# Where the head pieces and three attention units stand in the expert stages of a two-layer hybrid transformer kernel

## The chip, the cores and the metric

The kernel runs on one core of a Trainium2 chip, in one launch. The metric is the device time of that core in microseconds (us), lower is better. TensorE multiplies and transposes, VectorE and ScalarE work elementwise and empty the PSUM banks, GpSimd does a few powers and masks, and a queue of its own issues the transfers.

## The reference

Four sequences of 256 tokens of width 256 pass through eight residual blocks, each behind a layer norm:

```python
x = x + L0_attn_a(norm(x))   # 16 heads, causal softmax attention on a latent key/value
x = x + L0_ffn(norm(x))      # experts: top 2 of 8, shared W1/W3/W2 with a low-rank part per expert
x = x + L0_attn_b(norm(x))   # per token, softmax over the 16 heads of the same token
x = x + L0_ffn(norm(x))      # the experts again
x = x + L1_attn_a(norm(x))   # gated delta rule (linear attention)
x = x + L1_ffn(norm(x))      # gelu
x = x + L1_attn_b(norm(x))   # 16 heads, causal attention, one key/value head
x = x + L1_ffn(norm(x))
```

The parts that matter here are `L0_ffn` (gated product `silu(x W1 + lora) * (x W3 + lora)`, once per chosen expert slot), `L0_attn_b` (`scores[s, h, t] = q[s, h] . k[s, t]` for the 16 heads of one token, softmax over `t`, then a weighted sum of the 16 value rows) and `L0_attn_a`.

## The kernel before

All data of one sequence stays in SBUF. The work is cut into named stages such as `x_first` or `head_scores`. `program` calls the stages in one order written out by hand, and each engine walks that same order and issues only its own instructions of each stage. So every engine's queue is in order, and a stage's place decides what is queued behind it on every engine that has a part in it. Semaphores tie the engines together. PSUM has 8 banks. `lanes` tells which of them a stage may claim, and a claim waits until the bank's last user has drained it.

`experts(stage, k, s, beside)` computes the experts of sequence `s`. FT is 7. For step m = 0 to 8 it runs `x_first` m (m < 7), then the stages placed at slot `f<m>`, then `x_second` m-2 (m > 1), then (inside `middle`, from m = 4) `down_sum`, then the stages placed at slot `m`. `x_first` m is 16 TensorE instructions into a bank, a silu on ScalarE (line 1317) and a product on VectorE (line 1713). `x_second` m adds 8 TensorE instructions to the same bank and has a silu and a product of its own, and that product frees the bank. Two silu buffers are used in turn, so the silu of one product waits for the product two before it. After step 8 come `down` 1 0 (slot `down10`) and `down` 1 1, 14 TensorE instructions each; `down` 1 0 needs the products of all `x_second`.

`token_heads(s)` places `L0_attn_b` of another sequence beside those experts: `norm_t` 2 (transposes of the normed rows, waiting for VectorE's norm), `heads_in` (TensorE projects q, k, v; VectorE rotates them, lines 1755 to 1763), then 16 pieces of VectorE work. Pieces 0 to 7 are `head_scores` (a 128x1024 product and a 128x1024 sum, lines 1770 and 1771), pieces 8 to 15 are `head_mix` (lines 1787 and 1788). Pieces 3 and 7 end the scores of a token tile: they add a maximum and a subtraction (1774, 1775) and an Exp on ScalarE (1339). Pieces 8 and 12 start with a sum and a reciprocal (1785, 1786), and 11 and 15 end with a scaling (1791). `head_out_t` at slot `down10` waits for piece 15. There are four such stages, two per call of `middle`: the heads of the even sequences 0 and 2 beside the first-layer experts of 1 and 3, and the heads of the odd sequences 1 and 3 beside the second experts of 0 and 2. In the even ones the call order ahead is `x_first` 0, `lora`, `norm_x` 2, `experts`; in the odd ones other work lies between `norm_x` 2 and `norm_t` 2. `x_first` has banks 0 to 3 here.

The border half is one call of `experts` for sequence 2 (c) beside the four attention units of sequence 3 (d): `scores` (TensorE, maxima on VectorE, 8 Exp instructions on ScalarE, line 1266), `weights` (12 transposes, copies by VectorE and ScalarE), `values`, `values_t`. There `x_first` has only banks 0 to 2, so `x_first` m+1 waits for the product of `x_second` m-2, and sequence d uses banks 3 to 7. Exp and silu need different tables on ScalarE, so each change between them has a table load.

Of the kernel before, what the change touches and what calls it, by code (L numbers as in the profile page):

```python
# [97 lines left out]
def hybrid_kernel(nc, x_in, masks, packs, where, out):  # L98
    with ExitStack() as ctx:
# [319 lines left out]
        def program(stage):  # L419
# [24 lines left out]
            a, b, c, d = range(4)  # L444
# [15 lines left out]
            for other in (("scores", 0, (d, 0)), ("weights", 0, (d, 0)), ("spread_t", 0, c), ("top_exp", 0, c),  # L460
# [1 line left out]
                          ("gates", 0, c)):  # L462
                stage(*other)
            experts(stage, 0, c, {"f1": [("weights", 0, (d, 1))],
                                  "f2": [("values", 0, (d, 1)), ("scores", 0, (d, 2))],
                                  2: [("values_t", 0, (d, 1))], "f3": [("weights", 0, (d, 2))],
                                  3: [("values", 0, (d, 2)), ("scores", 0, (d, 3))],
                                  "f4": [("values_t", 0, (d, 2))], 4: [("weights", 0, (d, 3))],
                                  "f5": [("values", 0, (d, 3))], 5: [("values_t", 0, (d, 3))],
                                  6: [("out_in", 0, d)], 7: [("out_proj", 0, d), ("norm_x", 1, d)],  # L470
                                  "down00": [("norm_t", 1, d), ("router", 0, d), ("top_exp", 0, d), ("gates", 0, d)],
                                  "down01": [("spread_t", 0, d)], "down10": [("spread", 0, d), ("spread2", 0, d)]})
            halves[0] = False
# [23 lines left out]
        def middle(stage, a, b):  # L497
# [3 lines left out]
            stage("lora", 0, a)  # L501
            stage("norm_x", 2, a)
            experts(stage, 0, b, token_heads(a))
            stage("router", 1, a)
            stage("lora", 0, b)
# [5 lines left out]
            stage("x_first", 1, (a, 0))  # L511
            stage("gates", 1, a)
            experts(stage, 1, a, token_heads(b))
            stage("router", 1, b)
            stage("lora", 1, a)
# [50 lines left out]
        def token_heads(s):  # L566

            pieces = [("head_scores", 0, (s, a, h)) for a in range(NT) for h in range(HP)] \
                + [("head_mix", 0, (s, a, h)) for a in range(NT) for h in range(HP)]
            beside = {"f0": [("norm_t", 2, s)], 0: [("heads_in", 0, s)]}  # L570
            slots = ["f1", 1, "f2", 2, 2, "f3", 3, "f4", 4, 4, "f5", 5, 5, "f6", 6, 7]
            for slot, piece in zip(slots, pieces):
                beside.setdefault(slot, []).append(piece)
            beside["down10"] = [("head_out_t", 0, s), ("head_out", 0, s), ("norm_x", 3, s)]
            beside["down11"] = [("norm_t", 3, s)]
            return beside

        def experts(stage, k, s, beside):

            def others(slot):  # L580
                for b in beside.get(slot, ()):
                    stage(*b)

            for m in range(FT + 2):
                if m < FT and (m or (k == 0 and s % 2 == 0)):
                    stage("x_first", k, (s, m))
                others(f"f{m}")
                if m >= 2:
                    stage("x_second", k, (s, m - 2))
                if weave[0] and m >= 4:  # L590
                    summing[0] = True
                    for n in range(0 if m == 4 else m - 2, m - 1):
                        stage("down_sum", k, (s, n))
                others(m)
            for i in range(TOPK):
                for a in range(NT):
                    stage("down", k, (s, i, a))
                    others(f"down{i}{a}")
            summing[0] = False
            stage("lora_t", k, s)  # L600
# [69 lines left out]
        def _(pe):  # L670
# [554 lines left out]
            def stage(name, k, s):  # L1225
                seq = s if isinstance(s, int) else s[0]
                ring.lane = lanes(name, k, seq)
                table[name](k, s)

            program(stage)  # L1230


        @block.scalar
        def _(act):
# [259 lines left out]
            act.dma_start(pk[1][:, :], packs[1]).then_inc(loaded[1], 16)  # L1494
            act.dma_start(raw, masks).then_inc(masks_loaded, 16)
            program(lambda name, k, s: table[name](k, s))


        @block.vector
        def _(dve):  # L1500
# [586 lines left out]
            for s in range(S):  # L2087
                dve.memset(Vp[s][:, :, :, HD:HD + 1], 1.0).then_inc(prep, 1)
                dve.memset(Vp[s][:, :, :, HD + 1:PW], 0.0).then_inc(prep, 1)

            program(lambda name, k, s: table[name](k, s))


# [185 lines left out]
```

## Time and profile before

| | before |
|---|---|
| median of 3 runs | 1358.17 us (1352.16 to 1358.5) |
| profiled execution, its own time | 1358.74 us |
| its span | 1356.6 us |
| TensorE busy | 1214.7 us, 90% |
| VectorE busy | 747.1 us, 55% |
| ScalarE busy | 416.3 us, 31% |
| mean granted TensorE clock | 0.974 |

The span is the stretch that the profiler recorded; the execution's own time is 2.1 us longer. Busy shares are means over stages with different limits. An idle time in a timeline row stands in brackets with the engine that ended it. Ends of pipelined matmuls are modelled, so lengths of TensorE work are best read from start to start.

### The profile page before, as it was taken

To read this page: it belongs to the slowest core of one execution; us is meant where nothing else is said; L and a number is where in the kernel's file an instruction comes from. 1 tells how busy PE (TensorE), PEld (TensorE's weight loads), DVE (VectorE), ACT (ScalarE), POOL (GpSimd) and SP (SyncE) were. 2 spreads that over 40 slices of the span, in tenths; PEclk is the share of its full clock that TensorE was granted. 3 is DMA by queue.
4 is the path that set the end of the run, shared out by engine and by line. 5 is a ranking of instruction groups with operands and counts; after the bars stand their busy time and mean duration, and the time that the engine had idled before them with its cause. 6 is when DMAs were issued, how large, how long until landed. Compare 5 with 4: busy or idle time off the path is not lost.

```text
span 1356.6 us, 17608 instructions
## 1 busy us (share of the span) xinstructions
PE 1214.7 (90%) x6865; PEld 920.4 (68%) x6865; DVE 747.1 (55%) x1725; ACT 416.3 (31%) x897; POOL 79.7 (6%) x69
## 2 busy tenths in 40 slices
PE   6889898989999999978787898989989999999788
PEld 5577474766867778767665774756658777787666
DVE  5743387795456446444634333886964474564452
ACT  3522020222322343333453421212213322433352
POOL 0000000000110120010000000000002102200100
PEclk9999898999999989999998999999989999999999
DMA  8200000000000000000000000000000000000000
GB/s 351 98 1 0 0 1 0 1 0 0 1 0 1 1 1 1 1 1 9 1 8 1 0 1 0 0 1 0 0 1 1 1 0 1 0 1 2 1 1 16
DMA packets 3569, 17.32 MB, mean 13 GB/s; under 512 B 288, under 2 KB 2464, under 8 KB 2976
## 3 DMA queue, kind: packets, MB, share of 16 engines
q1 hardware_dynamic: 2912, 14.12, 2.6%
q10 hardware_dynamic: 576, 2.08, 0.4%
q8 instruction: 55, 0.90, 0.3%
q14 instruction: 26, 0.21, 0.0%
HBM read 15.15 MB, written 1.05 MB: 12 GB/s over the span
## 4 chain that ended last, share of the span: by engine, by line
PE 58%; DVE 22%; issue 9%; ACT 7%; POOL 3%; DMA 0%; DVEq 0%; POOLq 0%; ACTq 0%
PE bank L672 53%; ACT scr L1266 3%; DVE scr L1771 3%; DVE scr L1770 2%; DVE scr L1788 2%; PE bank L689 2%; DVE scr L1787 2%; DVE XnT L1944 1%; DVE scr L1713 1%; DVE XnT L1946 1%; DVE scr L1540 1%; DVE stat L1532 1%; POOL rstd L2100 1%; ACT L1317 1%; DVE negmax L1622 1%
## 5 line engine op out<-in xcount | busy, mean ns | idle before, releaser
L672 PE MATMUL bank<-pack,scr 128*128 128x512 f32 (+2 forms) x944 | 310.7, 481 | 8.5 <-ACT scr L1244 7.5
L672 PE MATMUL bank<-XnT,pack 128*128 128x256 f32 x1024 | 257.4, 392 | 16.5 <-ACT XnT L1244 7.1
L672 PEld LDWEIGHTS bank<-pack,scr 128*128 128x128 f32 x944 | 177.2, 192 | 115.6 <-issue 90.7
L672 PE MATMUL bank<-scr,pack 128*128 128x256 f32 x944 | 234.9, 390 | 19.3 <-DVE scr L1713 18.0
L672 PEld LDWEIGHTS bank<-XnT,pack 128*128 128x128 f32 x1024 | 195.5, 195 | 51.9 <-ACT XnT L1244 9.6
L672 PEld LDWEIGHTS bank<-scr,pack 128*128 128x128 f32 x944 | 182.7, 195 | 51.6 <-DVE scr L1713 21.3
L1713 DVE TENSOR_TENSOR scr<-bank,scr 128x256 f32<-128x256 f32 x112 | 47.3, 424 | 118.3 <-ACT scr L1317 116.0
L1266 ACT ACTIVATE scr<-bank,negmax 128x256 f32<-128x256 f32 (+1 forms) x256 | 82.9, 445 | 92.8 <-DVE negmax L1622 92.8
L1317 ACT ACTIVATE scr<-bank 128x256 f32<-128x256 f32 x112 | 42.1, 384 | 215.9 <-PE bank L672 155.1
L1244 ACT ACTIVATE scr<-bank 128x512 f32<-128x512 f32 (+7 forms) x112 | 51.0, 474 | 186.1 <-PE bank L689 91.6
L1620 DVE TENSOR_REDUCE negmax<-bank 128x2 f32<-128x512 f32 x64 | 43.8, 684 | 70.0 <-PE bank L672 70.0
L2100 POOL TENSOR_TENSOR rstd<-veps,half 128x2 f32<-128x2 f32 x32 | 22.3, 698 | 993.2 <-DVE veps L1537 993.2
L672 PE MATMUL bank<-scr 32*128 32x128 f32 (+4 forms) x944 | 77.5, 319 | 1.3 <-ACT scr L1244 1.3
L672 PEld LDWEIGHTS bank<-scr 32*128 32x128 f32 (+2 forms) x944 | 64.5, 183 | 19.0 <-issue 8.1
L1244 ACT ACTIVATE mats<-bank 128x512 f32<-128x512 f32 (+1 forms) x80 | 42.6, 555 | 106.1 <-PE bank L1077 83.2
L1525 DVE TENSOR_TENSOR X<-bank,X 128x512 f32<-128x512 f32 x31 | 21.4, 691 | 91.6 <-PE bank L672 91.6
L689 PE MATMUL bank<-pack,scr 128*128 128x128 f32 x232 | 37.9, 291 | 31.8 <-DVE scr L1540 23.5
L672 PE MATMUL bank<-identb 128*128 128x512 bf16 x197 | 55.1, 381 | 6.7 <-DVE scr L1644 5.6
L689 PEld LDWEIGHTS bank<-pack,scr 128*128 128x128 f32 x232 | 28.4, 149 | 47.8 <-issue 29.5
L790 PE MATMUL bank<-pack,scr 128*128 128x128 f32 x384 | 52.7, 285 | 8.2 <-ACT scr L1266 7.6
L672 PE MATMUL bank<-pack,XnT 128*128 128x8 f32 (+5 forms) x224 | 52.7, 377 | 5.1 <-ACT XnT L1244 5.1
L790 PEld LDWEIGHTS bank<-pack,scr 128*128 128x128 f32 x384 | 43.9, 145 | 14.4 <-ACT scr L1266 11.6
(179 smaller groups left out, 1406.1 us busy)
## 6 DMA issues: line engine op xcount, KB each, us to landing
pack<-pack_dram SPq DMA_DIRECT2D x1, 6152.0 KB, 17.2
pack<-pack_dram SPq DMA_DIRECT2D x1, 2180.0 KB, 29.7
pack<-pack_dram SPq DMA_DIRECT2D x1, 1595.0 KB, 23.7
X<-x SPq DMA_DIRECT2D x4, 256.0 KB, 17.1
pack<-pack_dram SPq DMA_DIRECT2D x1, 1024.0 KB, 20.6
pack<-pack_dram ACTq DMA_DIRECT2D x1, 975.5 KB, 6.2
pack<-pack_dram SPq DMA_DIRECT2D x1, 793.5 KB, 25.2
out_dram<-X SPq DMA_DIRECT2D x3, 256.0 KB, 2.1
```

The source lines that it names most:

```text
L672: return pe.matmul(o, l, r, start=start, stop=stop, skip_group_check=True)
L689: last = pe.transpose(o[:, t * T + a * P:t * T + a * P + P], src(t, a), ident)
L790: last = pe.transpose(o[:, (c - 4 * b) * P:(c - 4 * b + 1) * P], prob[s][:, u % PR, c * P:(c + 1) * P], ident)
L1244: act.activation(dst, src, func, **kw).then_inc(drain_of(key), 1)
L1266: ins = act.activation(prob[s][:, u % PR, j * HW + lo:j * HW + hi], psum(key, BANK)[:, lo:hi], ACT.Exp, bias=negmax[s][:, u % PR, tile, j: ...
L1317: act.activation(silu_x[s][:, n % SX, :], psum(key, T), ACT.Silu).then_inc(silu_ready[s], 1)
L1620: dve.tensor_reduce(negmax[s][:, u % PR, 1, 2 * h:2 * h + 2], o[:, :, P:HW], AX.X, ALU.max, negate=True).then_inc(max_ready[s], 1)
L1713: dve.tensor_tensor(x2T[s][:, i, m, :], psum(key, 2, T)[:, 1, :], silu_x[s][:, n % SX, :], ALU.mult)\
L1770: link(dve.tensor_tensor(prod[s][:, hh], *qk_pairs(s, a, hh), ALU.mult))
L1771: link(dve.tensor_reduce(sc[s][:, a, hh], prod[s][:, hh], AX.X, ALU.add))
L1787: link(dve.tensor_tensor(prod[s][:, hh], *pv_pairs(s, a, hh), ALU.mult))
L2100: return pool.tensor_tensor(dst, src, half[:, 0:1].broadcast_to(shape) if len(shape) == 2 else half[:, 0:1].unsqueeze(1).broadcast_to(shap ...
```

## The change

In `token_heads`, even sequences get `norm_t` and `heads_in` two steps later (slots `f2` and 2 in place of `f0` and 0), and their 16 pieces stand in slots 2 to 8 in place of `f1` to 7. Odd sequences keep `norm_t` and `heads_in`, and pieces 0 to 8 stand half a step earlier, piece 0 at slot 0; pieces 9 to 15 keep their slots. In the border half `values` and `scores` of units 1 and 2 move behind `x_second`, and the later units, `out_in`, `out_proj` and `norm_x` 1 move back by about half a step to a step. No instruction is added or removed.

```diff
--- before.py
+++ after.py
@@ -462,12 +462,12 @@
                           ("gates", 0, c)):
                 stage(*other)
             experts(stage, 0, c, {"f1": [("weights", 0, (d, 1))],
-                                  "f2": [("values", 0, (d, 1)), ("scores", 0, (d, 2))],
-                                  2: [("values_t", 0, (d, 1))], "f3": [("weights", 0, (d, 2))],
-                                  3: [("values", 0, (d, 2)), ("scores", 0, (d, 3))],
-                                  "f4": [("values_t", 0, (d, 2))], 4: [("weights", 0, (d, 3))],
-                                  "f5": [("values", 0, (d, 3))], 5: [("values_t", 0, (d, 3))],
-                                  6: [("out_in", 0, d)], 7: [("out_proj", 0, d), ("norm_x", 1, d)],
+                                  2: [("values", 0, (d, 1)), ("scores", 0, (d, 2))],
+                                  "f3": [("values_t", 0, (d, 1))], 3: [("weights", 0, (d, 2))],
+                                  "f4": [("values", 0, (d, 2))], 4: [("scores", 0, (d, 3)),  ("values_t", 0, (d, 2))],
+                                  5: [("weights", 0, (d, 3))],
+                                  "f6": [("values", 0, (d, 3))], 6: [("values_t", 0, (d, 3))],
+                                  7: [("out_in", 0, d)], 8: [("out_proj", 0, d), ("norm_x", 1, d)],
                                   "down00": [("norm_t", 1, d), ("router", 0, d), ("top_exp", 0, d), ("gates", 0, d)],
                                   "down01": [("spread_t", 0, d)], "down10": [("spread", 0, d), ("spread2", 0, d)]})
             halves[0] = False
@@ -567,8 +567,12 @@
 
             pieces = [("head_scores", 0, (s, a, h)) for a in range(NT) for h in range(HP)] \
                 + [("head_mix", 0, (s, a, h)) for a in range(NT) for h in range(HP)]
-            beside = {"f0": [("norm_t", 2, s)], 0: [("heads_in", 0, s)]}
-            slots = ["f1", 1, "f2", 2, 2, "f3", 3, "f4", 4, 4, "f5", 5, 5, "f6", 6, 7]
+            if s % 2 == 0:
+                beside = {"f2": [("norm_t", 2, s)], 2: [("heads_in", 0, s)]}
+                slots = [2, 2, "f3", 3, 3, "f4", 4, 4, "f5", 5, 5, "f6", 6, "f7", 7, 8]
+            else:
+                beside = {"f0": [("norm_t", 2, s)], 0: [("heads_in", 0, s)]}
+                slots = [0, "f1", 1, "f2", 2, 2, "f3", 3, "f4", 4, "f5", 5, 5, "f6", 6, 7]
             for slot, piece in zip(slots, pieces):
                 beside.setdefault(slot, []).append(piece)
             beside["down10"] = [("head_out_t", 0, s), ("head_out", 0, s), ("norm_x", 3, s)]
```

## Rows read from the trace of the kernel before

**Rows 1.** The page, part 4: engines' shares of the chain that ended last.

```profile
PE 58%; DVE 22%; issue 9%; ACT 7%; POOL 3%; DMA 0%; DVEq 0%; POOLq 0%; ACTq 0%
```

**Rows 2.** Timeline, TensorE, first even head stage: start, length (us), line, operation, shape, count [idle before].

```profile
153.75 1.89 PE L672 MATMUL bank<-pack,scr 128*128 128x256 f32 x8
159.53 1.09 PE L689 MATMUL bank<-pack,scr 128*128 128x128 f32 x4 [3.89 <-DVE scr L1540]
161.30 7.04 PE L672 MATMUL bank<-pack,XnT 128*128 128x512 f32 x16 [0.69 <-ACT XnT L1244]
...
214.23 3.78 PE L672 MATMUL bank<-scr,pack 128*128 128x256 f32 x8 [4.51 <-DVE scr L1713]
217.81 8.58 PE L672 MATMUL bank<-pack,scr 128*128 128x512 f32 x18
226.22 0.60 PE L689 MATMUL bank<-pack,scr 128*128 128x128 f32 x4
```

**Rows 3.** Timeline, VectorE, the same stage.

```profile
172.66 1.22 DVE L1770 TENSOR_TENSOR scr<-scr 128x1024 f32<-128x1024 f32 x1
...
175.16 1.22 DVE L1770 TENSOR_TENSOR scr<-scr 128x1024 f32<-128x1024 f32 x1
...
198.26 0.42 DVE L1713 TENSOR_TENSOR scr<-bank,scr 128x256 f32<-128x256 f32 x1 [2.18 <-ACT scr L1317]
...
222.28 0.42 DVE L1791 TENSOR_TENSOR scr<-scr,bmax 128x256 f32<-128x256 f32 x1
```

**Rows 4.** Timeline, ScalarE, the same stage, behind the eighth score piece.

```profile
196.54 1.28 ACT L1317 ACT_TABLE_LOAD   x1
197.84 0.66 ACT L1317 ACTIVATE scr<-bank 128x256 f32<-128x256 f32 x2
```

**Rows 5.** Timeline, TensorE, first odd head stage.

```profile
251.01 5.43 PE L672 MATMUL bank<-pack,XnT 128*128 128x512 f32 x16 [0.69 <-ACT XnT L1244]
256.28 1.03 PE L672 MATMUL bank<-XnT,pack 128*128 128x256 f32 x4
257.14 1.03 PE L672 MATMUL bank<-scr,pack 128*128 128x256 f32 x4
...
302.33 3.78 PE L672 MATMUL bank<-scr,pack 128*128 128x256 f32 x8 [4.51 <-DVE scr L1713]
...
314.64 0.60 PE L689 MATMUL bank<-pack,scr 128*128 128x128 f32 x4
```

**Rows 6.** Timeline, VectorE, the same odd stage.

```profile
260.42 0.42 DVE L1713 TENSOR_TENSOR scr<-bank,scr 128x256 f32<-128x256 f32 x1 [2.06 <-ACT scr L1317]
...
310.72 0.42 DVE L1713 TENSOR_TENSOR scr<-bank,scr 128x256 f32<-128x256 f32 x1
```

**Rows 7.** Busy time by stretch: us, engines' busy time, then the granted clock (PEclk).

```profile
214.00:216.00 2.00, 1.77 (x4) 1.50 (x5) 1.97 (x3) 0.38 (x1) 0.00 (x0) 0.50 0.00 0
722.00:730.00 8.00, 5.46 (x35) 4.43 (x34) 6.59 (x25) 0.60 (x1) 0.70 (x1) 1.00 0.00 1
734.00:740.00 6.00, 3.82 (x30) 2.46 (x30) 3.33 (x6) 3.69 (x10) 0.00 (x0) 0.83 0.00 0
```

**Rows 8.** Timeline, TensorE, expert stage beside the last L0 attention.

```profile
757.63 0.61 PE L672 MATMUL bank<-negb,identb 128*128 128x256 bf16 x4
...
759.04 1.99 PE L672 MATMUL bank<-scr,pack 128*128 128x256 f32 x8
...
765.20 1.99 PE L672 MATMUL bank<-XnT,pack 128*128 128x256 f32 x4 [3.95 <-DVE scr L1713]
...
790.07 1.13 PE L672 MATMUL bank<-XnT,pack 128*128 128x256 f32 x4 [0.71 <-DVE scr L1713]
...
800.98 6.17 PE L672 MATMUL bank<-pack,scr 128*128 128x512 f32 x14
```

**Rows 9.** Timeline, ScalarE, the same stage, third unit's exponentials.

```profile
760.39 2.60 ACT L1266 ACTIVATE scr<-bank,negmax 128x256 f32<-128x256 f32 x8 [0.94 <-DVE negmax L1622]
763.01 1.28 ACT L1317 ACT_TABLE_LOAD   x1
```

## Prediction

> **What bounds the kernel now.** I read the page's chain first: TensorE holds 58% of it and VectorE 22% [rows 1]. So the time is mostly TensorE's own work, and what can be won is the time in which TensorE waits. The timelines of TensorE then show where it waits inside the stages that the diff touches, and those of VectorE and ScalarE show why. In the first even head stage TensorE waits twice. It stands 3.89 us before the transposes of `norm_t` 2, because VectorE's norm follows `lora` directly, and 0.69 us for ScalarE's copy. It stands 4.51 us before `x_second` 6, for the product of `x_first` 6, which lies in VectorE's queue behind 13 head pieces [rows 2]. From piece 0 at 172.66 to the end of piece 15 at 222.70 VectorE stands still only once, for 2.18 us behind the Exp of piece 7 [rows 3], so late in the stage VectorE sets the pace. The odd stage has the second wait, 4.51 us, and 0.69 us at its start [rows 5]; VectorE also stands 2.06 us between the rotation and the product of `x_first` 1 [rows 6]. The other two head stages repeat the pair (3.90 and 4.50 us in the even one, 4.50 in the odd one). The border half has waits of 3.95 and 0.71 us before `x_first` 3 and 6, both for the product of an `x_second` that frees a bank [rows 8].
>
> **The clock adds to each long wait.** Behind the 4.51 us the granted clock is 0.50 of full speed, 1.2 instead of 2.4 GHz [rows 7], and eight instructions take 3.58 us start to start [rows 2] where eight at full speed take 1.73: four take 0.86 [rows 5]. `heads_in` takes 7.04 us behind the 3.89 us wait [rows 2] and 5.43 (5.27 start to start) in the odd stage without such a wait [rows 5].
>
> **The even stages.** Nothing is added or removed; only the queues' order changes, with no transfer in it. Unit prices: `x_first` 4 x 0.86 = 3.45 us, `x_second` 1.73, `heads_in` 5.27, transposes of `norm_t` about 0.4 [rows 2, 5], 0.43 for each 512-wide instruction, 6.0 for the 14 of a `down` [rows 8], 2.50 for a head piece [rows 3]. TensorE ends `lora` at 155.64 [rows 2]. It now goes on with `x_first` 1 and 2 until 162.5; the normed rows are there since about 159.5, so neither the transposes nor (behind `x_second` 0, which covers ScalarE's copy) `heads_in` wait. `heads_in` starts at 155.64 + 3.45 + 3.45 + 0.4 + 1.73 = 164.7. The rotation ends 7.35 us after the start of `heads_in`: 260.42 - 2.06 - 251.01 [rows 5, 6]. That gives 172.05 for the start of piece 0, against 172.66 [rows 3]. From there to the end of piece 15 VectorE before had 11 products among the pieces; now it has ten (those of `x_first` 2 and `x_second` 0 are done before, that of `x_second` 6 joins), so 50.04 - 0.42 = 49.6 us. Piece 3 is followed by piece 4 in its slot, which covers its Exp; piece 7 is again followed by a product, so the one 2.18 us stall stays. Piece 15 ends at 221.7.
>
> TensorE on the other side comes to `x_second` 6 at about 202.7 and waits there some 3.9 us for the product of `x_first` 6 (piece 10 ends at 206.2), probably at half clock behind it, and reaches the end of `down` 1 0 at about 220.1, held by the product of `x_second` 6 at 219.3. Then `head_out_t` is late next: it waits for piece 15 until 221.7. Before it started at 226.22 [rows 2]. So each even stage wins 226.22 - 221.7 = 4.5 us, although TensorE's waits don't vanish. VectorE's slower bound hides what TensorE loses to the clock up to that point. Two stages: 9.0 us. Bounds: 4.5 each if the clock is full at `head_out_t`; if it has fallen there, `head_out` and `down` 1 1 run slow, and a slow stretch costs 1.6 us (7.04 against 5.43, [rows 2, 5]) to 2.6 us (12.31 against 9.7, worked out below). That leaves 1.9 to 4.5. I take 4.5, since TensorE works most of the 11 us before.
>
> **The odd stages.** Piece 0 at slot 0 fills VectorE's 2.06 us of idle time [rows 6]. But piece 3 moves from a place where piece 4 followed it to `f2`, where the product of `x_second` 0 follows. That product's silu stands behind the Exp of piece 3 in ScalarE's queue, and Exp, table load and silu cost VectorE 2.18 us, the price that the row behind piece 7 shows [rows 3]. Adding VectorE's queue up piece by piece with these prices, the product of `x_first` 6 comes 0.24 us later than before (2.50 + 2.18 - 2.06 and the differences of short overlaps, with the same 13 pieces ahead of it). So the order itself wins nothing. `x_first` 4 needs the bank that the product of `x_second` 0 frees, about 272.4, and TensorE is there at 270.1: a new wait of 2.3 us. It takes away from the wait later: before `x_second` 6 it is about 2.2 us in place of 4.51. That can spare the drop of the clock. Behind 302.33 `x_second` 6, `down_sum` and `down` 1 0 took 314.64 - 302.33 = 12.31 us [rows 5]; at full clock, held only by the product of `x_second` 6 at 310.72 + 0.24 [rows 6], they take 9.7. That is a gain of 2.3 us net (1.8 in the second odd stage, where the stretch is 11.80). If the clock falls anyway, the stage loses the 0.24. The rows do not decide: with 3.82 of 6 us busy from 734 the mean clock is 0.83, so it fell there; with 5.46 of 8 us busy from 722 it stayed 1.00 [rows 7]. I take the middle, 1.0 each, 2.0 us for both; bounds -0.5 and 4.1.
>
> The Trainium skill, "ScalarE: Activation LUTs", section "What ACT_TABLE_LOAD costs", gives a load of about 1283 ns and a drain of about 1380 ns more for every switch of table set. The load is the 1.28 of [rows 4], but the silu follows 0.02 us behind its end, so this trace has no such drain, and the measurement decides. With it the new stall would be 3.56 us.
>
> **The border half.** `values` and `scores` of unit 2 now stand between `x_second` 0 and `x_first` 3. They are 1.41 us of `scores` [rows 8] and some 0.8 of `values`, and the product they cover comes about 1.1 us behind the matmul (a silu of 0.4, 0.66 for two [rows 4], a product of 0.42 [rows 3], and the hops between engines), since the silu is no longer queued behind eight Exp and two table loads [rows 9]. So the wait of 3.95 us goes, and with it the half clock behind it: the four instructions behind the wait take 1.99 us where 1.03 to 1.13 is normal [rows 5, 8], and so do the next four: 1.8 us. `x_first` 6 has `weights` in front now and loses its 0.71. What could take their place is the Exp. It ends 3.95 us after the end of `scores` (762.99 against 759.04 [rows 8, 9]); TensorE has `x_first` 3, `values_t` and `x_second` 1, 5.5 us, in between, so `weights` 2 doesn't wait. The silu of `x_second` 1 is delayed by the table load to about 6.1 us after `scores`, its product ends at about 6.9, and `x_first` 4 wants it at 6.8: 0.1 to 0.2 us. Unit 3 repeats this with the same cover. `out_proj` ends 6 us (`down` 0 0, 6.0 [rows 8]) before `norm_t` 1, whose norm takes about 3.9 (the wait of [rows 2]). Sum 3.95 + 1.8 + 0.71 = 6.5 us; bounds 4.7 (two new waits of the size of the 0.71, no gain of clock lost) and 6.9.
>
> **Sum.** 9.0 + 2.0 + 6.5 = 17.5 us. The profiled execution of 1358.74 (span 1356.6) becomes 1341.2; it stands 0.6 over the median 1358.17, so the median becomes 1340.7. The stages behind each of these are released by TensorE or by chains that start from it, so I see nothing that eats the gain.
>
> **Rivals.**
> - The clock takes part of it back: it falls behind `head_out_t` in both even stages (2.1 us each, the middle of 1.6 and 2.6) and behind the last wait in both odd ones (0.24 lost in each). 6.5 + 9.0 - 4.2 - 0.5 = 10.8, so 1347.4. For it: TensorE has about five waits of 1 to 4 us in each head stage now. Against: each is shorter than those behind which the rows show half clock at length.
> - The delay of the heads doesn't pay: VectorE gets behind by as much as the front won, for instance because the rotation starts later than 164.7 allows. Then only the border half stands, 1351.7. For it: a second Exp stall of 2.18 us per even stage, with a later rotation, would do it. Against: the start of `heads_in` hangs on TensorE alone, whose `x_first` 1 and 2 wait for nothing that the rows show.
> - The new stall behind piece 3 is longer than 2.18 us. The longest wait that an Exp in a silu's way makes in these stages is the 3.95 us before `x_first` 3 [rows 8]. That is 1.77 more in each odd stage, 14.0 us of gain, 1344.2. Against: it has eight Exp instructions and two table loads in it. The rule of the Trainium skill, "ScalarE: Activation LUTs", section "What ACT_TABLE_LOAD costs", would make the stall 3.56, near this; [rows 4] speak against it.
> - Slower than before: in the even stages 9 us of other TensorE work now stand ahead of `heads_in`, and piece 15 ends directly ahead of `head_out_t`, with no cover left. So VectorE's lateness is paid one for one. With L us late in each even stage the time is 1340.7 + 2 L: level with before at L = 8.75, over 0.5% slower from 12.2, and 1366.7 at 13. That would take six uncovered Exp stalls of 2.18 us in each stage, and the order has one.
>
> **How the numbers follow.** As summed 0.55, clock 0.26, no pay of the heads 0.12, longer stall 0.04, slower 0.03. A measurement tells 0.5% (6.8 us) from no change. Faster by more takes the first, second and fourth and a quarter of the third, 0.88; within 0.5% 0.09; slower 0.03. The range goes from 1335 (all upper bounds, 9.0 + 4.1 + 6.9 = 20, and the runs' own spread of some 3 us below) to 1349 (the clock rival and 1 us).
>
> **What would show it.** In the even stages no wait ahead of `norm_t` 2, `heads_in` at 5.3 us, piece 0 some 0.6 us earlier and piece 15 ending with `head_out_t` right behind. In the odd stages a product of `x_second` 0 that waits 2.2 us for ScalarE, a TensorE wait before `x_first` 4, and the one before `x_second` 6 near 2.2 us. In the border half no wait over 0.3 us ahead of `x_first` 3 to 6. Wrong would be: VectorE idle twice in the even stages, half clock at `head_out`, or `weights` waiting for Exp.

## The result, and the profile after

| | before | after | after, second job |
|---|---|---|---|
| median | 1358.34 us (1352.16 to 1361.23) | 1338.71 us (1336.32 to 1340.25) | 1343.34 us (1342.4 to 1346.31), before 1358.4 beside it |
| ratio to before, 95% interval | | 0.9852 [0.9832, 0.9872] | 0.9887 [0.9871, 0.9904] |
| span of the profiled execution | 1356.6 us | 1334.2 us | 1344.2 us |
| mean granted TensorE clock | 0.974 | 0.988 | 0.976 |

The forecast was 1340.7 with a range of 1335 to 1349. A job is a group of runs measured together, with the kernel before beside them. The two jobs stand on either side of the forecast, 2.0 below and 2.6 above. The four runs of the changed kernel in the first job (1336.32 to 1340.25) and the four in the second (1342.4 to 1346.31) don't overlap, while the medians of the kernel before agree within 1.5 us over all four jobs (1358.34, 1359.03, 1358.4, 1359.81). Its two profiled spans are 10 us apart, and most of that lies in stages that the diff does not touch.

The line numbers of the changed kernel are 4 higher than those of before. The page's part 1 (busy time, share of the span, instructions) and part 4 (shares of the chain) of the changed kernel:

```profile
PE 1200.0 (90%) x6865; PEld 908.1 (68%) x6865; DVE 748.1 (56%) x1725; ACT 416.2 (31%) x897; POOL 79.7 (6%) x69
...
PE 55%; DVE 25%; issue 10%; ACT 7%; POOL 3%; DMA 0%; DVEq 0%; POOLq 0%; ACTq 0%
```

VectorE's share of the chain rose from 22% [rows 1] to 25%, TensorE's fell by 3 points: the head stages are now set by VectorE's pieces up to their end. TensorE's busy time fell by 14.7 us although it has the same 6865 instructions, so about two thirds of the 22.4 us by which the span is shorter is a faster clock, as far as modelled ends of matmuls can tell.

**The first even head stage.** Timeline of TensorE in the changed kernel (start, length in us, line, operation, shapes, count, idle before and its releaser), the rows that answer to [rows 2]:

```profile
161.38 0.60 PE L693 MATMUL bank<-pack,scr 128*128 128x128 f32 x4
161.82 1.89 PE L676 MATMUL bank<-scr,pack 128*128 128x256 f32 x8
163.55 5.32 PE L676 MATMUL bank<-pack,XnT 128*128 128x512 f32 x16
...
205.50 1.99 PE L676 MATMUL bank<-scr,pack 128*128 128x256 f32 x8 [3.88 <-DVE scr L1717]
207.33 6.17 PE L676 MATMUL bank<-pack,scr 128*128 128x512 f32 x14
214.90 1.13 PE L676 MATMUL bank<-pack,scr 128*128 128x512 f32 x2 [1.40 <-DVE scr L1717]
217.74 2.08 PE L676 MATMUL bank<-pack,scr 128*128 128x512 f32 x2 [1.72 <-DVE scr L1717]
220.59 1.12 PE L693 MATMUL bank<-pack,scr 128*128 128x128 f32 x4 [0.77 <-DVE scr L1795]
222.39 10.05 PE L676 MATMUL bank<-pack,scr 128*128 128x256 f32 x21 [0.69 <-ACT scr L1248]
```

No bracket stands at `norm_t` 2 or `heads_in`. `head_out_t` (220.59) waits for the last scaling of piece 15. Everything from the stage's start on lies 1.0 us earlier than before for a reason ahead of it, so 220.59 is 221.6 on the clock of before, where the forecast had 221.7. But from 217.74 on the work is slow. The windows of the changed kernel over this place (busy us and count of each engine, then the granted clock):

```profile
217.00:219.00 2.00, 1.26 (x2) 0.50 (x2) 1.93 (x4) 0.00 (x0) 0.00 (x0) 0.55 0.00 0
219.00:222.00 3.00, 1.93 (x5) 0.72 (x4) 2.86 (x6) 0.26 (x1) 0.00 (x0) 0.50 0.00 0
222.00:226.00 4.00, 3.61 (x9) 2.89 (x10) 1.28 (x3) 0.34 (x1) 0.00 (x0) 0.50 0.00 0
226.00:230.00 4.00, 4.00 (x9) 1.78 (x8) 2.69 (x8) 0.00 (x0) 0.69 (x1) 0.82 0.00 0
```

`head_out` runs at half clock up to about 227. From `head_out_t` to the transposes behind the stage (`lora_t`) it is 14.05 us, where before it was 11.05: 3.0 us given back. The second even stage shows 13.97, so 2.9.

**VectorE in both kinds of stage.** Its timeline in the changed kernel, rows that answer to [rows 3] and [rows 6]:

```profile
196.07 0.42 DVE L1717 TENSOR_TENSOR scr<-bank,scr 128x256 f32<-128x256 f32 x1 [2.18 <-ACT scr L1321]
...
255.76 1.23 DVE L1774 TENSOR_TENSOR scr<-scr 128x1024 f32<-128x1024 f32 x1
...
269.54 0.42 DVE L1717 TENSOR_TENSOR scr<-bank,scr 128x256 f32<-128x256 f32 x1 [2.18 <-ACT scr L1321]
```

The even stage keeps its one stall of 2.18 us. In the odd stage piece 0 follows the rotation at once (255.76), and the new stall behind piece 3 (269.54) is 2.18 us too.

**The first odd stage.** TensorE in the changed kernel, answering to [rows 5]:

```profile
270.02 1.13 PE L676 MATMUL bank<-XnT,pack 128*128 128x256 f32 x4 [2.40 <-DVE scr L1717]
...
287.70 1.13 PE L676 MATMUL bank<-XnT,pack 128*128 128x256 f32 x4 [0.20 <-DVE scr L1717]
...
299.95 1.99 PE L676 MATMUL bank<-scr,pack 128*128 128x256 f32 x8 [1.64 <-DVE scr L1717]
...
309.78 0.60 PE L693 MATMUL bank<-pack,scr 128*128 128x128 f32 x4
```

`x_first` 4 has a wait of 2.40 (forecast 2.3), the wait before `x_second` 6 is 1.64 (about 2.2), and behind it eight instructions take 1.99 us where they took 3.78. The clock stayed full, so the stretch to `head_out_t` is 9.83 us (9.7).

**The border half.** TensorE in the changed kernel, answering to [rows 8]:

```profile
748.52 1.13 PE L676 MATMUL bank<-XnT,pack 128*128 128x256 f32 x4
...
755.45 1.13 PE L676 MATMUL bank<-XnT,pack 128*128 128x256 f32 x4
...
768.58 1.47 PE L794 MATMUL bank<-pack,scr 128*128 128x128 f32 x12
...
780.16 7.90 PE L676 MATMUL bank<-pack,scr 128*128 128x256 f32 x22
```

No row between `x_first` 3 (748.52) and `norm_t` 1 (787.90) has a bracket at all. The half is 101.31 us long, from 108.14.

**The ledger.** `transposes` leaves 55 rows in every trace, at the same places of the program. Their starts cut each execution into stages that can be laid beside each other. The differences to before, in us, negative is shorter:

```
                         even 1  odd 1  border  even 2  odd 2   all other stages
before, second profile    -0.4    0.0     0.0     0.0    0.0       -0.4
after                     -1.6   -2.2    -6.8    -1.6   -1.7       -8.4
after, second job         -3.1   -2.2    -6.8    -1.6   -1.7       +3.0
even stages only          -4.6   -1.3     0.0    -1.6   +0.8       +4.6
odd stages only           -0.4   -2.2    +0.1    +0.1   -1.7       -1.9
border only               -0.4    0.0    -6.8     0.0    0.0       -0.3
```

The touched stages won 14.0 us where 17.5 were forecast. The untouched ones, which the forecast counted at nothing, won 8.4 us in this profile and lost 3.0 in the other.

The odd stages with their old order are not the same in every profile either: 88.4 and 87.9 us in before, 87.1 and 88.7 in the kernel with the even part alone, whose odd stages nobody changed. With the new order they took 86.2 us in all twelve cases (six profiles).

### The profile page after: what moved, and what is told of

It reads as the page before. It is cut to its first block, busy times and chain, and to the rows that moved or that the text cites. A ratio compares the mean times of both kernels' runs of the same rounds, so it can differ in the third digit from the quotient of the medians.

```text
span 1334.2 us, 17602 instructions
## 1 busy us (share of the span) xinstructions
PE 1200.0 (90%) x6865; PEld 908.1 (68%) x6865; DVE 748.1 (56%) x1725; ACT 416.2 (31%) x897; POOL 79.7 (6%) x69
## 4 chain that ended last, share of the span: by engine, by line
PE 55%; DVE 25%; issue 10%; ACT 7%; POOL 3%; DMA 0%; DVEq 0%; POOLq 0%; ACTq 0%
PE bank L676 51%; ACT scr L1270 3%; DVE scr L1775 3%; DVE scr L1774 3%; DVE scr L1792 2%; DVE scr L1791 2%; PE bank L693 2%; DVE XnT L1948 2%; DVE XnT L1950 1%; DVE scr L1717 1%; DVE scr L1759 1%; DVE scr L1544 1%; DVE stat L1536 1%; POOL rstd L2104 1%; DVE negmax L1626 1%
## 5 line engine op out<-in xcount | busy, mean ns | idle before, releaser
L676 PE MATMUL bank<-pack,scr 128*128 128x512 f32 (+2 forms) x944 | 316.7, 488 | 13.4 <-ACT scr L1248 7.5
L676 PE MATMUL bank<-XnT,pack 128*128 128x256 f32 x1024 | 250.8, 385 | 17.1 <-ACT XnT L1248 7.2
L676 PE MATMUL bank<-scr,pack 128*128 128x256 f32 x944 | 227.9, 381 | 12.3 <-DVE scr L1717 11.1
L676 PEld LDWEIGHTS bank<-XnT,pack 128*128 128x128 f32 x1024 | 191.0, 191 | 51.8 <-DVE scr L1717 10.5
L676 PEld LDWEIGHTS bank<-scr,pack 128*128 128x128 f32 x944 | 177.9, 190 | 42.8 <-DVE scr L1717 14.4
L794 PEld LDWEIGHTS bank<-pack,scr 128*128 128x128 f32 x384 | 43.0, 143 | 14.7 <-ACT scr L1270 11.9
L1248 ACT ACTIVATE XnT<-bank 128x512 f32<-128x512 f32 x32 | 19.4, 605 | 104.3 <-PE bank L693 104.1
```

What stands on the lines that cost most here:

```text
L676: return pe.matmul(o, l, r, start=start, stop=stop, skip_group_check=True)
L794: last = pe.transpose(o[:, (c - 4 * b) * P:(c - 4 * b + 1) * P], prob[s][:, u % PR, c * P:(c + 1) * P], ident)
L1248: act.activation(dst, src, func, **kw).then_inc(drain_of(key), 1)
```

## The experiments

**The kernel before once more, and the parts one by one.** The kernel before is unchanged in the first. Each of the others makes one part of the change and leaves the rest as before:

```diff
 # even stages only
+            if s % 2 == 0:
+                beside = {"f2": [("norm_t", 2, s)], 2: [("heads_in", 0, s)]}
+                slots = [2, 2, "f3", 3, 3, "f4", 4, 4, "f5", 5, 5, "f6", 6, "f7", 7, 8]
 # odd stages only
+            else:
+                slots = [0, "f1", 1, "f2", 2, 2, "f3", 3, "f4", 4, "f5", 5, 5, "f6", 6, 7]
 # border only: the dictionary of the border half's experts(...) as in the change
```

> The kernel before once more, for a second profile. Theory one: the granted clock of the stages from 315 to 714 us varies between executions of one kernel, so this profile's stretch from the transposes at 325.69 to those at 725.49 (399.8 us there, 390.5 in the changed kernel) differs by 2 us or more from 399.8. Rival: the stretch stays within 1 us of 399.8, and the shortening belongs to the change.

> Only the even head stages have their new order. Theory one (order plus clock, as the trace of the changed kernel shows it): head_out_t starts 4.6 us earlier in each even stage, but the clock falls right there and takes 3.0 back, so each stage wins 1.6 us up to lora_t, 3.2 us in all, 1355.1 us. Rival: the clock's fall there is chance, and the order is worth its full 9.2 us in most runs, 1349.1. Second rival: the 7 us that the changed kernel won between 315 and 714 us, in stages that the change does not touch, belong to this part; then 1348 or below, and the stretch from the second odd stage's end to the border half is 7 us shorter than in the kernel before.

> Only pieces 0 to 8 of the odd head stages have their new places. Theory one: VectorE gains 2.06 us and pays 2.18 us behind piece 3, the product of x_first 6 comes 0.2 us later, but TensorE's wait before x_second 6 shrinks from 4.5 to about 1.7 to 2.2 us and the clock stays at 2.4 GHz: 2.2 and 1.7 us won, 1354.4. Rival: the order is worth nothing without luck in the clock, -0.5 us, 1358.8.

> Only the attention units beside the experts of sequence 2 stand in their new places. Theory one: the waits of 3.95 and 0.71 us and the half clock behind the first go, 6.8 us, 1351.5. Rival: without the clock's part 4.7 us, 1353.7.

Measured against a before of 1359.03: before again 1357.91 (one run); even only 1356.52, 0.999 [0.997, 1.0011]; odd only 1351.68, 0.9959 [0.9929, 0.9989]; border only 1349.08, 0.9918 [0.9886, 0.9949]. The stage lengths say it more sharply than the medians: the border half is worth 6.84 us alone as in the whole, the odd stages 2.2 and 1.7. The medians won 2.5, 7.4 and 10.0 us (expected 1355.1, 1354.4 and 1351.5), the stages 6.2, 3.9 and 6.8; only one execution of each has a profile, so these differences are not located. The even part alone has the full 4.6 us in its first stage and 1.6 in its second, and in its profile lost 4.6 in stages that nobody touched. Its median cannot be told from before.

The kernel before, profiled a second time, went against its first theory. The stretch from 325.69 to 725.49, where the clock was thought to vary by chance, was 399.78 us in it, 399.81 in the border part alone and 399.80 in before: it repeats within 0.03 us as long as all ahead of it is unchanged. In every other kernel here it is shorter, 392.4 to 398.4 us (spare products in it not counted). So something ahead of the stretch moves its clock, though no instruction in it differs; this profile alone spoke for the rival, that the shortening belongs to the change. A second profile of the changed kernel, below, shows that its length varies by chance as well.

The first even stage of the even part shows what the order is worth when the clock does not fall late. TensorE in the kernel with the even part alone:

```profile
206.24 3.78 PE L676 MATMUL bank<-scr,pack 128*128 128x256 f32 x8 [3.88 <-DVE scr L1717]
209.81 7.99 PE L676 MATMUL bank<-pack,scr 128*128 128x512 f32 x16
218.49 1.12 PE L676 MATMUL bank<-pack,scr 128*128 128x512 f32 x2 [0.68 <-DVE scr L1717]
221.33 0.66 PE L693 MATMUL bank<-pack,scr 128*128 128x128 f32 x4 [1.72 <-DVE scr L1795]
222.67 8.00 PE L676 MATMUL bank<-pack,scr 128*128 128x256 f32 x22 [0.69 <-ACT scr L1248]
```

The same wait of 3.88 us as in the whole change, but here the clock fell directly behind it (3.78 us for eight, against 1.99). It was full again by `head_out` (22 in 8.00 us). Slow work at 206 costs nothing, since VectorE's queue sets `head_out_t`; slow work at 222 costs 3.0 us. So the order's gain is shown, and what is lost of it is where the clock falls.

The late fall is the rule, though, and not the exception. Five profiles have this even order without spare products or a covered piece 7 (the change twice, the even part alone, and two kernels further below that shift a later stage), ten even stages. From `head_out_t` to `lora_t` they took 11.11 us once, 12.59 once and 13.97 to 14.06 eight times. The rival that most runs would have the full 9.2 us is out.

**The change once more.**

> The changed kernel once more. Theory one (each untouched stage has two lengths, with the clock up or fallen, and which one comes depends on where the stage falls in time, so both can come for one kernel): time 1336 to 1343, and at least one of the stages between the transposes at 437.43 and 477.90 (40.5 us), 486.15 and 523.72 (37.6), 666.65 and 701.99 (35.3) may come out at the longer value that the kernel before shows there (43.6, 39.3, 36.9). Rival: all three repeat within 0.2 us.

1343.34, 0.9887 [0.9871, 0.9904], just over the expected 1336 to 1343. All three named stages came out longer than in the first profile, so the rival is out: 41.92 us in place of 40.47 (before has 43.56), 39.30 in place of 37.57 and 36.97 in place of 35.34. The last two are the lengths of before, the first is a third length. The stretch that repeated in before (399.8 us) was 398.20 us here and 392.41 in the first profile. So it does vary between executions of the changed kernel. All touched stages but the first even one repeat within 0.03 us. That one won 3.1 us in place of 1.6: the clock had fallen early, as above, and fell again for a part of `head_out`. TensorE in the second profile of the changed kernel:

```profile
206.55 3.78 PE L676 MATMUL bank<-scr,pack 128*128 128x256 f32 x8 [3.88 <-DVE scr L1717]
...
222.99 9.48 PE L676 MATMUL bank<-pack,scr 128*128 128x256 f32 x22 [0.69 <-ACT scr L1248]
```

9.48 us for the 22 that took 8.00 at full clock. The rest of the difference between the two profiles is in untouched stages. Windows of nearly the same stretch of work (it begins 0.35 us earlier in the second), first in the first profile, then in the second:

```profile
465.00:478.00 13.00, 12.17 (x85) 10.19 (x85) 7.44 (x16) 6.98 (x16) 2.26 (x1) 1.00 0.01 1
478.00:491.00 13.00, 10.48 (x58) 7.57 (x57) 6.48 (x19) 4.42 (x9) 6.43 (x4) 1.00 0.00 1
```

```profile
465.00:478.00 13.00, 12.17 (x75) 10.64 (x75) 7.31 (x17) 6.16 (x15) 2.31 (x2) 0.87 0.00 1
478.00:491.00 13.00, 10.48 (x49) 7.06 (x48) 6.25 (x17) 3.62 (x6) 6.38 (x4) 0.92 0.00 1
```

No instruction differs, only the clock, 1.00 against 0.87 and 0.92.

**The clock at head_out held by spare products.** The kernel has a helper that issues bf16 products whose result nothing reads. Here they fill the waits of the even stages' end. The cut leaves out that the bank of `down` 1 0 is claimed early, for the first of these products to write to:

```diff
 def x_second ...
+                if early(k, s, m):          # k == 0, odd s, m == 6
+                    warm(claim(pe, ("down", r, 1, 0)), 14)
 def down ...
+                if (i, a) == (1, 0) and early(k, s):
+                    warm(o, 6)
 def head_out_t ...
-                pe.wait_ge(bctx_ready[s], nth(s, 1, 1))
-                transposes(("bctxT", s), ..., KD)
+                transposes(("bctxT", s), ..., KD,
+                           0 if s % 2 else 6, (bctx_ready[s], nth(s, 1, 1)))
```

> The changed kernel with spare bf16 products on TensorE in the waits of the even head stages (14 before x_second 6, 6 before down 1 0, 6 before head_out_t), all inside waits of 3.9, 1.4 to 1.7 and 0.8 to 1.7 us. Theory one (the half clock behind head_out_t takes back 3.0 us per even stage): head_out_t to lora_t takes 11.1 us in place of 14.0 in both, 5.9 us won, 1332.8. Rival: the stage is bound by VectorE behind head_out_t too, or the spare products delay TensorE, 1338.7 or more.

1338.58, 0.9846 [0.9826, 0.9866]. TensorE in this kernel, first even stage:

```profile
218.64 1.94 PE L676 MATMUL bank<-pack,scr 128*128 128x512 f32 x2 [1.72 <-DVE scr L1728]
220.38 2.38 PE L676 MATMUL bank<-identb 128*128 128x512 bf16 x6
222.59 0.60 PE L693 MATMUL bank<-pack,scr 128*128 128x128 f32 x4
223.88 8.00 PE L676 MATMUL bank<-pack,scr 128*128 128x256 f32 x22 [0.69 <-ACT scr L1259]
```

From `head_out_t` (222.59) to `lora_t` (233.64) it is 11.05 us again, to the hundredth what before had, and 11.11 in the second even stage. The 3.0 us were the clock. Part of the gain is spent, though. The six spare products ran at half clock (2.38 us) and held `head_out_t` back by about 1 us. The two even stages won 3.5 and 4.4 us against before, 8.0 in place of 3.2. That is 4.8 us more than in the first profile of the change, where 5.9 were expected, and the medians of the job that both share are 4.8 apart (1343.34 and 1338.58). The expected 1332.8, counted from the other job's median, was missed.

**The Exp covered by one more piece.** An Exp ahead of the silu that the next product needs costs 2.18 us. In the first of these kernels a further piece stands in the same slot behind piece 3 and behind piece 7 of all four stages, so that VectorE works through the Exp; the rest is the change. The second has it behind piece 3 of the odd stages alone, and otherwise the kernel before:

```diff
-                slots = [2, 2, "f3", 3, 3, "f4", 4, 4, "f5", 5, 5, "f6", 6, "f7", 7, 8]
+                slots = [2, 2, "f3", 3, 3, "f4", 4, 4, 4, "f5", 5, "f6", 6, "f7", 7, 8]
-                slots = [0, "f1", 1, "f2", 2, 2, "f3", 3, "f4", 4, "f5", 5, 5, "f6", 6, 7]
+                slots = [0, "f1", 1, 2, 2, 2, "f3", 3, 3, "f4", 4, "f5", 5, "f6", 6, 7]
 # the second kernel, odd stages
+                slots = [0, "f1", 1, 2, 2, 2, "f3", 3, "f4", 4, "f5", 5, 5, "f6", 6, 7]
```

> The changed kernel with a piece put directly behind pieces 3 and 7 in both kinds of head stage, so that no Exp of a score tile stands uncovered. Theory one (each uncovered Exp costs VectorE 2.18 us): one stall less in each even stage, head_out_t 2.2 us earlier; two stalls less in each odd stage, and TensorE's waits of 2.4, 0.2 and 1.6 us there go, 4.2 us. 12.8 us in all, 1325.9, and up to 6 us more if the clock now stays up at head_out_t. Rival: the stalls were hidden behind TensorE's own work, less than 4 us, 1335 or more.

> The kernel before with the new odd placing, but pieces 3 to 5 in slot 2, so that piece 4 covers the Exp of piece 3; even stages and border half as before. Against the run with the new odd placing alone (profile 1350.5 span, median 1351.7) theory one expects VectorE 2.2 us earlier, no wait before x_first 4, the wait before x_second 6 about 1.9 us, and 2.2 us less in each odd stage, 1347.3. Rival: the stall behind piece 3 costs TensorE nothing net, since it has time later, 1351.7.

All four: 1333.24, 0.9821 [0.9805, 0.9838]. The odd stages are 82.00 us each, 4.2 less than in the change. TensorE in this kernel, first odd stage, the rows around the last product of the experts; the wait before `x_second` 6 is gone:

```profile
283.07 1.13 PE L676 MATMUL bank<-XnT,pack 128*128 128x256 f32 x4 [0.84 <-DVE scr L1717]
...
293.51 1.89 PE L676 MATMUL bank<-scr,pack 128*128 128x256 f32 x8
295.24 7.89 PE L676 MATMUL bank<-pack,scr 128*128 128x512 f32 x18
302.96 0.60 PE L693 MATMUL bank<-pack,scr 128*128 128x128 f32 x4
```

The even stages are 83.06 and 82.95 us; `head_out` is still slow there (22 in 9.96 us). The four stages together are 14.0 us shorter than in the first profile of the change (12.8 expected), but the untouched ones are 7.4 longer, and the median is 10.1 us under the change's of the same job. The expected 1325.9 was missed. Odd stages alone: 1350.22, 0.9959 [0.9941, 0.9977]; each is 83.94 us, 2.26 less than in the change, which is the one stall of 2.18. So, by the stages, the new stall was what kept the odd part small. The medians (1350.22 here, 1351.68 with the uncovered order in another job; 1347.3 was expected) don't tell the two apart.

**Does the time at which a stage begins set its clock?** One untouched stage, from the 18th to the 19th of the 55 rows, had been 43.56 us long where it began at 441.5 to 442.3, and 40.47 where it began at 437.4. To move its beginning alone, spare products (5, and 22) were put into an earlier stage of the changed kernel:

```diff
 def x_first ...
+                if (k, s, m) == (1, 1, 1):
+                    warm(o, 5)     # 22 in the second kernel
```

> The changed kernel with 5 spare bf16 products (1.1 us) ahead of x_first 1 in the third expert stage, so that all later stages arrive 1.1 us later. Theory one (the length of an untouched stage goes by when it arrives; in the profiles so far the stage that starts with the transposes near 437 took 40.5 us for arrivals of 437.4 to 440.7, 42.0 for 436.3 to 437.1, 43.6 for 441.5 to 442.3): arrival 438.2 to 438.5 and 40.5 us. Rival: the clock's falls there are chance, and any of the three lengths comes. Time: 1.1 us more than the changed kernel and a few us of luck, 1335 to 1346.

> The same with 22 spare products (4.7 us). Theory one: arrival at 441.9 to 442.2 and the slow length of 43.6 us in that stage, as in both profiles of the kernel before, 1343 to 1350. Rival: any length; if it is 40.5, the arrival does not decide.

1343.34, 0.9887 [0.9859, 0.9915], and 1345.78, 0.9905 [0.9879, 0.9932]. The stage came out otherwise than the theory had it, both times. With 5 it began at 438.83 and took 41.99 us, with 22 at 442.44 and took 41.91. All profiles together, in order of the beginning:

```
began at   428.2 430.4 430.6 436.3 436.5 437.1 437.4 437.6 438.8 440.7 441.5 441.7 442.3 442.4
us long    41.99 40.46 40.47 41.99 41.99 41.92 40.47 40.47 41.99 40.46 43.56 43.56 43.56 41.91
```

There are three lengths (within 0.08 us), and the time since the span's start doesn't choose among them. The theory falls. What chooses stays open. All three cases of 43.56 are kernels with nothing changed ahead of this stage.

**Both together.** The pieces of the kernel with all four stages covered, and the spare products of the even stages with smaller counts (6, 6 and 7), so that they end before the work they wait for:

> Pieces 3 and 7 covered in all head stages, and spare bf16 products in the waits of the even ones (6 before x_second 6, 6 before down 1 0, 7 before head_out_t). Theory one: the covered order's gain and the clock kept behind head_out_t add up, so the even stages take 81 us (83.0 with the cover alone, 87.4 before) and the time is 4 us under the covered kernel alone, 1329. Rival: the spare products run at half clock in their turn and delay head_out_t by as much as they save, 1333.

> The covered order once more, beside the other three, for the comparison in one job. Theory one: 1330 to 1336, head stages of 83.0 and 82.0 us again. Rival: the first run of it was a lucky one, 1338 or more.

Against a before of 1359.81: both together 1324.2, 0.9744 [0.9726, 0.9763]; the covered kernel again 1332.71, 0.9822 [0.9789, 0.9855]. Both together is the fastest kernel of the study, well clear of the change in either job. The covered kernel beat the change in the job that they shared (0.9821 against 0.9887); against the change's first job (0.9852) its two intervals overlap or touch. TensorE in the kernel with both, end of the first even stage, and its windows:

```profile
215.60 1.13 PE L676 MATMUL bank<-pack,scr 128*128 128x512 f32 x2 [1.72 <-DVE scr L1728]
216.56 1.67 PE L676 MATMUL bank<-identb 128*128 128x512 bf16 x7
218.44 0.66 PE L693 MATMUL bank<-pack,scr 128*128 128x128 f32 x4 [0.21 <-DVE scr L1806]
219.79 8.00 PE L676 MATMUL bank<-pack,scr 128*128 128x256 f32 x22 [0.69 <-ACT scr L1259]
```

```profile
218.00:222.00 4.00, 3.10 (x15) 2.23 (x14) 3.11 (x8) 0.60 (x1) 0.00 (x0) 1.00 0.00 0
222.00:226.00 4.00, 4.00 (x11) 1.80 (x10) 2.60 (x8) 0.00 (x0) 0.70 (x1) 1.00 0.00 0
```

The even stages are 80.63 and 80.62 us, 2.3 less than with the covers alone, and the clock is 1.00 through `head_out`. These 4.6 us are what the spare products are shown to win. The medians are 8.5 us apart and the profiled spans only 2.6, since other stages took 2.0 us more in this profile; no stage accounts for the rest of the medians' difference. The stages came as expected (81 us; 83.0 and 82.0 for the covered order), and the median 1324.2 is 5 us better than the 1329 expected.

## Why the prediction was right, and where it was not

**The even stages' order: right.** Forecast 4.5 us each up to `head_out_t`. From the stage's start to `head_out_t` it was 76.42 us and is 71.79, so 4.6. The parts agree one by one: no wait at `norm_t` 2, `heads_in` 5.32 us, one stall of 2.18, 3.88 us before `x_second` 6 (3.9).

**The even stages' clock: the step that failed, and one of the signs of being wrong that the prediction named.** The prediction took "4.5, since TensorE works most of the 11 us before" `head_out_t`, and "if it has fallen there" a slow stretch of 1.6 to 2.6 us. It had fallen, and cost 3.0 and 2.9 us. Net 1.6 each, under the lower bound of 1.9. The prediction had expected half clock early, behind the 3.9 us, where VectorE hides it. In the first profile it held there and fell at the second of three shorter waits in a row, 1.40, 1.72 and 0.77 us, the last of them right at `head_out_t`. The first rival had this mechanism in the even stages, too cheap at 2.1. Its other half, a fall of the clock behind the last wait of the odd stages, didn't come. In the kernel with the odd part alone the clock fell behind the new wait before `x_first` 4 (a granted clock of 0.76 from 273 to 280 us), and the stage took 86.20 us all the same: a fall that VectorE's queue hides. That the full 4.5 can be had is shown by the first even stage of the even part alone (4.6).

**The odd stages: mechanism right, size too small.** Stall 2.18 us, wait at `x_first` 4 2.40 us, and the clock full behind the shortened last wait: 2.2 and 1.7 us, where 2.3 and 1.8 had been worked out for that case and 1.0 each was taken as the middle. The term was 3.9 us, not 2.0. The third rival, a longer stall, is out: 2.18 us in the changed kernel too. The delay of 0.24 us for the product of `x_first` 6 was right (0.25), although the three numbers in its bracket add up to 2.62: the same 13 pieces stand ahead, so 2.50 has no place there. In the change itself piece 4 keeps its slot 2, and the other eight of pieces 0 to 8 move; this is why piece 3 lost its cover.

The rule of the Trainium skill, "ScalarE: Activation LUTs", section "What ACT_TABLE_LOAD costs", of a drain on top of the load, would have made this stall 3.56 us. The changed kernel's 2.18 us speaks against it here, as the trace of before had.

**The border half: right.** 6.8 us against 6.5, in every kernel that has it, and no new wait of any size. Its bounds were less well founded. Two new waits of 0.71 us would leave 5.0, not 4.7, which is the sum without the clock's 1.8 us; the upper bound of 6.9 has no working.

**The second rival and the slower case** don't hold: the heads' delay pays 4.6 us up to `head_out_t`, and VectorE was not late.

**The sum.** 2 x 1.6 + 3.9 + 6.8 = 14.0 us in the touched stages (17.5 forecast). The sentence "I see nothing that eats the gain" left out that the clock of stages that nobody touched can change: 8.4 us for the change in the first profile, 3.0 against it in the second. So the nearness of 1338.71 to 1340.7 is in part luck: what was missing in the even stages was made up elsewhere. Between the two jobs' medians, 19.6 and 15.1 us were won; what the change itself does to its stages is 14.0 to 15.4.

What is only argued: that the untouched stages' clock explains the medians' difference between the jobs. It is read from one profile each, and why the runs of the two jobs don't overlap is open. What puts an untouched stage on 40.5, 42.0 or 43.6 us was not found.

## What to carry to other kernels

In a hand-ordered kernel with in-order queues, price a reordering by adding up the slowest engine's queue piece by piece. Here that gave the waits it named within 0.6 us and the stages' own gain, clock apart, within a few tenths. Then ask of each wait that stays not only how long it is but what stands behind it. Here a fall of the clock ahead of a later wait was free, and the same fall at the last dependent stretch was paid in full (3.0 us); spare products that fitted in the waits won 2.3 us of it in each even stage. When an Exp stands ahead of a silu that the next product needs, put one more independent piece of VectorE work directly behind the piece that calls the Exp. And compare stage by stage against two profiles of each kernel, since stages with identical instructions moved by 8.4 us in all, and 11.4 between two executions of one kernel.

## What the runs showed of the hardware

- The same stretch, at the same wait of 3.88 us, was followed by full clock in one execution (eight instructions 1.99 us) and by half clock in another of the same kernel (3.78 us). In the first, half clock came at the second of the waits of 1.40, 1.72 and 0.77 us that followed.
- An untouched stage had three lengths, 40.5, 41.9 to 42.0 and 43.6 us, with granted clocks of 1.00 down to 0.83 in it, and its beginning in the span did not tell which. The Trainium skill, "TensorE: Matmul & The Clock Gate", section "Part 1: The HAM clock gate (the "warmup" mystery)", says that the gate runs free of the program, so that one kernel shows other counts of slow products from run to run. The two profiles of the changed kernel agree with it: 40.47 and 41.92 us for this stage, 1334.2 and 1344.2 us in all. The kernel before does not show it: in its two profiles and in the border part alone the stage took 43.56 us each time.
